# Cross-attention and a gated expert layer on one core: four late sums move from VectorE to ScalarE, one small load moves last, and all engine orders are rewritten

## The reference

```python
h  = layernorm(x)                                   # no affine part
q, k, v = h @ Wq.T + bq, ctx @ Wk.T + bk, ctx @ Wv.T + bv   # 16 heads of 32
p  = softmax(clip(q k^T / sqrt(32), -50, 50), masked)
d  = clip(rs, 0, 0.3) * ((p v) @ Wo.T + bo)         # rs: one number
x1 = x + layernorm(d) * gamma + beta
n  = layernorm(x1)
gate = top2 of softmax(n @ router.T)                # 8 experts
out  = x1 + sum_e gate_e * (silu(n @ down_e.T) @ up_e.T)    # 16 hidden features each
```

## Time and profile before

| | us |
|---|---|
| median of 3 runs | 186.54 (184.55 to 188.71) |
| profiled execution | 186.6 |
| its span, first to last instruction | 183.9 |
| TensorE busy in it | 171.8 |
| VectorE, ScalarE, GpSimd busy | 137.5, 113.4, 101.8 |
| DMA bytes read, written | 19.95 MB, 9.96 MB |

### The profile page before, as it was taken

The page is one execution under the profiler, slowest core; times in us unless marked ns, Lnnn a source line. Parts: engine busy times, 40 slices in busy tenths (PEclk is TensorE's granted clock), DMA queues, the critical chain, the costliest instruction groups (busy, mean ns, idle before and its releaser), DMA issues.

```text
span 183.9 us, 3557 instructions
## 1 busy us (share of the span) xinstructions
PE 171.8 (93%) x1212; PEld 126.2 (69%) x1212; DVE 137.5 (75%) x306; ACT 113.4 (62%) x231; POOL 101.8 (55%) x157
## 2 busy tenths in 40 slices
PE   7999779979998899999999999989999999999990
PEld 7486558846654378884888486666778598889860
DVE  3788498997999558998238584467898898773993
ACT  3038706984853875489986592769734787778410
POOL 5032089995837528999966984416133595364100
PEclk9999999999999999999999999999999999999999
DMA  6999995000157596455991526430409458000248
GB/s 168 354 384 300 399 250 207 4 0 4 62 150 279 136 284 172 124 179 204 302 215 67 173 59 197 148 95 18 114 18 329 127 221 235 4 2 0 86 176 309
DMA packets 18049, 30.13 MB, mean 164 GB/s; under 512 B 3056, under 2 KB 8176, under 8 KB 17776
## 3 DMA queue, kind: packets, MB, share of 16 engines
q1 hardware_dynamic: 18032, 29.92, 51.5%
HBM read 19.95 MB, written 9.96 MB: 163 GB/s over the span
## 4 chain that ended last, share of the span: by engine, by line
PE 44%; DVE 23%; DMA 13%; SPq 8%; issue 4%; POOL 3%; ACT 3%; DVEq 0%; ACTq 0%
PE ps L469 38%; DMA xs<-x 6%; DMA rz_scratch<-rz 3%; DVE xs L1223 3%; PE ps L574 3%; DVE stage L1147 3%; DVE ln_st L1231 3%; DVE hst_lo L1088 2%; DMA x_scratch<-x_turned 2%; PE ps L560 2%; DVE v_sb L1132 2%; POOL attt_lo L1509 2%; DMA wk<-rz_scratch 1%; SPq L360 1%; DVE wk L1157 1%
## 5 line engine op out<-in xcount | busy, mean ns | idle before, releaser
L1509 POOL TENSOR_TENSOR attt_lo<-wk,attt_hi 128x512 fp32r<-128x512 f32 x16 | 21.7, 1373 | 13.6 <-ACT attt_hi L801 13.5
L469 PE MATMUL ps<-hst_hi,wq_hi 128*128 128x512 f32 x64 | 26.2, 409 | 2.3 <-DVE hst_lo L1088 2.3
L469 PE MATMUL ps<-wo_hi,attt_hi 128*128 128x512 f32 x64 | 25.9, 405 | 0.2 <-POOL attt_lo L1509 0.2
L1505 POOL TENSOR_TENSOR xs<-xs,beta_bc 128x512 f32<-128x512 f32 x16 | 20.7, 1320 | 9.4 <-DMA beta_bc<-beta 8.1
L469 PE MATMUL ps<-hst_hi,wq_lo 128*128 128x512 f32 x64 | 25.3, 395 | 0.0
L469 PE MATMUL ps<-wo_hi,attt_lo 128*128 128x512 f32 x64 | 25.3, 395 | 0.0
L469 PE MATMUL ps<-wo_lo,attt_hi 128*128 128x512 f32 x64 | 25.3, 395 | 0.0
L469 PE MATMUL ps<-hst_lo,wq_hi 128*128 128x512 f32 x64 | 25.2, 394 | 0.0
L764 ACT ACTIVATE hs<-xs,ln_bias,ln_rstd 128x512 f32<-128x512 f32 x16 | 12.1, 807 | 11.5 <-POOL ln_bias L1497 11.5
L783 ACT ACTIVATE stage<-ps 128x1024 f32<-128x1024 f32 x16 | 15.9, 1025 | 5.3 <-PE ps L546 5.3
L1147 DVE TENSOR_SCALAR stage<-stage,exp_max 128x1024 f32<-128x1024 f32 x16 | 15.3, 959 | 5.1 <-ACT stage L783 5.1
(11 more groups left out here) (111 smaller groups left out, 387.6 us busy)
## 6 DMA issues: line engine op xcount, KB each, us to landing
wk<-rz_scratch SPq DMA_DIRECT2D x32, 128.0 KB, 2.8
out<-xs SPq DMA_DIRECT2D x16, 256.0 KB, 2.2
xs<-x SPq DMA_DIRECT2D x3, 1024.0 KB, 8.9
x_scratch<-x_turned SPq DMA_DIRECT2D x6, 512.0 KB, 2.6
x_turned<-x_scratch SPq DMA_DIRECT2D x24, 128.0 KB, 2.9
hs_scratch<-hs_turned SPq DMA_DIRECT2D x2, 1024.0 KB, 5.1
hs<-hs_scratch SPq DMA_DIRECT2D x8, 256.0 KB, 5.4
wk<-wk_t SPq DMA_DIRECT2D x4, 256.0 KB, 5.9
```

Of the source, the lines that this page charges most:

```text
L469: last = pe.matmul(dst, w, m, start=start and i == 0, stop=stop and i == n - 1, skip_group_check=unseen)
L1505: pool.tensor_tensor(xt, xt, beta_bc[:, :], ALU.add).then_inc(xb_ok, 1)
L1509: pool.tensor_tensor(attt_lo[:, :, c, :], att[:, c, :].rearrange("p (t n) -> p t n", t=NT), attt_hi[:, :, c, :].bitcast(F32), ALU.subtract ...
```

## The change

Four tiles, (2,1), (2,3), (3,1) and (3,2), get another way to their last sum. ScalarE copies x1 into the bank of the tile's experts (`experts_seed`, a use of kind `E` in `BANKS`), the three matmuls of `up` add to what is there, and ScalarE copies the sum back to SBUF (its own `finish`). VectorE no longer calls `finish` for them. The load of rs becomes `rs_load` and is issued as the last of the first loads; `residual_scale` stands later on VectorE. The other loads after `x1_load` come in another order, `load(3)` is issued before `hs_fetch(2)`, and the orders of all five engines and the uses of the banks are rewritten. No matmul, and no other computation, is added or taken away.

The part of the orders between those shown follows the same pattern: batch 0's experts (`down`, `hid_transpose`, `up`, `largest`, `gating`) come earlier on all engines, and `scores(1, 1)`, `sums(1, 1)` and `project(1, ...)` come later. On TensorE the sequence there is `project(0, 0)`, `(0, 1)`, `(0, 2)`, `sums(1, 0)`, `weigh(1, 0)`, `project(0, 3)`, `query(2, 0)`, `(2, 1)`, `down(0, 0)`, `(0, 1)`, `scores(1, 1)`, `query(2, 2)`, `scores(2, 0)`, `query(2, 3)`, `hid_transpose(0, 0)`, `sums(1, 1)`, `sums(2, 0)`, `up(0, 0)`, `(0, 1)`, `down(0, 2)`, `(0, 3)`, `weigh(1, 1)`, `scores(2, 1)`, `query(3, 0)`, `(3, 1)`, `hid_transpose(0, 1)`, `sums(2, 1)`, `project(1, 0)` to `(1, 3)`, `query(3, 2)`, `weigh(2, 0)`, `scores(3, 0)`, `weigh(2, 1)`, `query(3, 3)`, `down(1, 0)`, `(1, 1)`, `sums(3, 0)`, `scores(3, 1)`, `weigh(3, 0)`, `project(2, 0)`, `(2, 1)`, `sums(3, 1)`, `hid_transpose(1, 0)`, `project(2, 2)`, `down(1, 2)`, `(1, 3)`, `project(2, 3)`, `weigh(3, 1)`, `up(0, 2)`, `(0, 3)`, `hid_transpose(1, 1)`, `up(1, 0)`, `(1, 1)`, `down(2, 0)`, `(2, 1)`, `project(3, 0)`, `(3, 1)`, `hid_transpose(2, 0)`, `project(3, 2)`.

```diff
-    "K0 Q01 S02 S06 S10 Q13 W00 Q21 Q23 W12 S26 S30 W20 U01 U10 W33 U22 U33",
-    "K1 Q02 S03 S07 S11 S16 W03 S20 W10 W13 S27 S31 S34 W21 U02 W31 U20 U31",
-    "K2 Q03 S04 Q11 Q12 S17 Q20 S21 W11 Q30 S32 S35 W22 U11 U12 U23",
-    "K3 S00 S05 S12 S14 W01 Q22 S22 S24 Q31 S33 S36 W23 W30 U13 U30",
-    "h00 h02 Q00 S01 Q10 S13 S15 W02 S23 S25 Q32 Q33 S37 U00 U03 W32 U21 U32",
-    "V0 h11 m0 v02 v10 v13 v21 f01 f02 a00 v31 a01 v33 f20 a20 n30 f30 f32 a30",
-    "V1 h12 s00 v00 v03 v11 f00 s20 s21 v23 s30 v30 f11 v32 f12 f21 f22 n31 f31 f33 a31",
-    "h01 h03 h10 h13 s01 v01 s10 s11 v12 v20 v22 f03 s31 f10 a10 f13 a11 f23 n32 n33 a21",
+    "K0 Q02 Q03 Q10 S12 W03 Q22 Q23 S26 W11 S30 S34 W21 U03 W31 E31",
+    "K1 S00 S04 Q11 S13 Q20 S14 S20 U00 S27 W12 S31 S35 W22 U10 W32 U12 E32",
+    "K2 S01 S05 Q12 Q13 W02 S15 S21 U01 Q30 W13 S32 S36 W23 U11 W33 U13 U20 U22",
+    "K3 S02 S06 S10 W00 Q21 S16 S22 S24 Q31 Q32 S33 S37 E21 U30",
+    "h00 h02 Q00 Q01 S03 S07 S11 W01 S17 S23 S25 W10 Q33 W20 U02 W30 E23 U33",
+    "V0 h11 m0 v01 s10 f00 a00 f02 v13 v20 v23 s30 s31 f12 v33 f21 f22 n31 f31 f32 a30",
+    "V1 h12 s00 s01 v02 v10 f01 s20 v12 s21 v21 f10 v30 a10 f13 a11 f23 n32 a21",
+    "h01 h03 h10 h13 v00 v03 v11 s11 f03 a01 v22 f11 v31 v32 f20 a20 n30 f30 n33 f33 a31",
 )
 MOVED = ((0, 0), (0, 1), (1, 0), (1, 1), (2, 0), (2, 1))
+
+UP_ON_SCALAR = ((2, 1), (2, 3), (3, 1), (3, 2),)
 MOVED_HS = (2, 3,)
...
+e_seeded, e_full, e_free = sem("e_seeded"), sem("e_full"), sem("e_free")
...
+def rs_load():
     sp.dma_start(rs_raw[:, :], rs.broadcast_to([P, 1])).then_inc(rs_in, 16)
...
 def store(b, t):
-    sp.wait_ge(u_free, banks.count(f"U{b}{t}"))
+    if (b, t) in UP_ON_SCALAR:
+        sp.wait_ge(e_free, banks.count(f"E{b}{t}"))
+    else:
+        sp.wait_ge(u_free, banks.count(f"U{b}{t}"))
     sp.dma_start(out_tiles[:, bass.ds(NT * b + t, 1), :],
...
# SyncE's order
 small_load()
 x1_load()
+bv_load()
+experts_load()
+wo_load()
+load(2)
 gamma_load()
-wo_load()
 bo_load()
-experts_load()
-bv_load()
-load(2)
+rs_load()
 spread_out(0, 0)
 spread_in(0, 0)
 spread_out(0, 1)
# TensorE's up(b, t), then its order
-    dst = take(f"U{b}{t}")
-    passes(dst, three(hidt_hi[:, t, :], hidt_lo[:, t, :], up_hi[:, :], up_lo[:, :])
-           ).then_inc(u_full, 1)
+    weights = three(hidt_hi[:, t, :], hidt_lo[:, t, :], up_hi[:, :], up_lo[:, :])
+    if (b, t) in UP_ON_SCALAR:
+        pe.wait_ge(e_seeded, banks.count(f"E{b}{t}"))
+        passes(bank(f"E{b}{t}"), weights, start=False, unseen=True).then_inc(e_full, 1)
+    else:
+        passes(take(f"U{b}{t}"), weights).then_inc(u_full, 1)
 values(0)
+keys(0)
 values(1)
-keys(0)
-keys(1)
 hs_transpose(0, 0)
 hs_transpose(0, 1)
-values(2)
+keys(1)
 keys(2)
-values(3)
 hs_transpose(0, 2)
 hs_transpose(0, 3)
+values(2)
+values(3)
+query(0, 0)
 keys(3)
-query(0, 0)
 query(0, 1)
 query(0, 2)
+scores(0, 0)
 query(0, 3)
 hs_transpose(1, 0)
 hs_transpose(1, 1)
-scores(0, 0)
 hs_transpose(1, 2)
+scores(0, 1)
 hs_transpose(1, 3)
 expert_means()
-scores(0, 1)
+sums(0, 0)
 query(1, 0)
-sums(0, 0)
+weigh(0, 0)
 sums(0, 1)
 query(1, 1)
-weigh(0, 0)
-scores(1, 0)
 query(1, 2)
 weigh(0, 1)
+scores(1, 0)
 query(1, 3)
-sums(1, 0)
-scores(1, 1)
-weigh(1, 0)
 project(0, 0)
-sums(1, 1)
 project(0, 1)
...
 project(3, 0)
 project(3, 1)
-hid_transpose(1, 1)
 hid_transpose(2, 0)
 project(3, 2)
+project(3, 3)
+up(1, 2)
 down(2, 2)
 down(2, 3)
-project(3, 3)
+up(1, 3)
 x1_transpose(3, 0)
 x1_transpose(3, 1)
 x1_transpose(3, 2)
 down(3, 0)
 down(3, 1)
+hid_transpose(2, 1)
 x1_transpose(3, 3)
 down(3, 2)
 down(3, 3)
-up(1, 2)
-up(1, 3)
-hid_transpose(2, 1)
 up(2, 0)
 up(2, 1)
 hid_transpose(3, 0)
# ScalarE: new functions, then the end of its order
+def experts_seed(b, t):
+    before = banks.before(f"E{b}{t}")
+    act.wait_ge(x1_ok, NT * b + t + 1)
+    act.wait_ge(freeing[before[0]], banks.count(before))
+    act.copy(bank(f"E{b}{t}"), xs[:, NT * b + t, :]).then_inc(e_seeded, 1)
+
+def finish(b, t):
+
+    act.wait_ge(e_full, banks.count(f"E{b}{t}"))
+    act.copy(xs[:, NT * b + t, :], bank(f"E{b}{t}")).then_inc(e_free, 1)
+
 def projected_squares(b, t):
...
+projected_squares(3, 2)
 x1_out(2, 3)
-projected_squares(3, 1)
-hid_hi(1, 1)
-hid_hi(2, 0)
-x1_squares(3, 0)
-projected_squares(3, 2)
+x1_squares(3, 1)
+experts_seed(3, 1)
+x1_squares(3, 2)
+projected_squares(3, 3)
+experts_seed(3, 2)
 down_scaled(2, 2)
-x1_squares(3, 1)
 down_scaled(2, 3)
 hidden_tanh(2, 1)
+x1_out(3, 0)
 exp_logits(2, 1)
-x1_squares(3, 2)
-projected_squares(3, 3)
-x1_out(3, 0)
 x1_out(3, 1)
 x1_out(3, 2)
 x1_squares(3, 3)
 down_scaled(3, 0)
 down_scaled(3, 1)
-x1_out(3, 3)
 hidden_tanh(3, 0)
 exp_logits(3, 0)
+x1_out(3, 3)
 down_scaled(3, 2)
+hid_hi(2, 1)
 down_scaled(3, 3)
 hidden_tanh(3, 1)
-hid_hi(2, 1)
 exp_logits(3, 1)
 hid_hi(3, 0)
+finish(2, 1)
+finish(2, 3)
 hid_hi(3, 1)
+finish(3, 1)
+finish(3, 2)
# VectorE's order: start and end
-clean_finite(1)
 tile_stats(0, 0)
 tile_stats(0, 1)
+clean_finite(1)
+tile_stats(0, 2)
+tile_stats(0, 3)
 clean_marks(2)
-tile_stats(0, 2)
 clean_limited(2)
+hs_lo(0, 0)
 clean_finite(2)
 clean_marks(3)
-tile_stats(0, 3)
-hs_lo(0, 0)
+clean_limited(3)
 hs_lo(0, 1)
-clean_limited(3)
+clean_finite(3)
 wq_low(0)
-clean_finite(3)
 wq_low(1)
+hs_lo(0, 2)
+hs_lo(0, 3)
 wq_low(2)
 wq_low(3)
+tile_stats(1, 0)
 mask_limits()
-residual_scale()
-tile_stats(1, 0)
-hs_lo(0, 2)
-hs_lo(0, 3)
 tile_stats(1, 1)
 tile_stats(1, 2)
 tile_stats(1, 3)
-centre_wo(0)
-centre_wo(1)
-centre_wo(2)
 value_blocks(0)
 value_blocks(1)
 tile_stats(2, 0)
 tile_stats(2, 1)
 tile_stats(2, 2)
+residual_scale()
+centre_wo(0)
+centre_wo(1)
+centre_wo(2)
+clip(0, 0)
+clip(0, 1)
 hs_lo(1, 0)
 hs_lo(1, 1)
-clip(0, 0)
 hs_lo(1, 2)
 hs_lo(1, 3)
...
 scaled(3, 0)
 residual(3, 0)
-hid_lo(1, 1)
 hid_lo(2, 0)
 scaled(3, 1)
 residual(3, 1)
 scaled(3, 2)
 residual(3, 2)
+finish(1, 2)
+scaled(3, 3)
+residual(3, 3)
+finish(1, 3)
 largest(2, 1)
 gating(2, 1)
-scaled(3, 3)
-residual(3, 3)
 largest(3, 0)
 gating(3, 0)
-finish(1, 2)
+hid_lo(2, 1)
 largest(3, 1)
-finish(1, 3)
-hid_lo(2, 1)
+finish(2, 0)
 gating(3, 1)
 hid_lo(3, 0)
-finish(2, 0)
-finish(2, 1)
+finish(2, 2)
 hid_lo(3, 1)
-finish(2, 2)
-finish(2, 3)
 finish(3, 0)
-finish(3, 1)
-finish(3, 2)
 finish(3, 3)
```

423 lines of the change are left out of this document (217 added, 206 removed).

## The result

The changed kernel took **191.34 us** (median of 4 runs, 189.45 to 194.77) beside 186.7 for the kernel before: ratio 1.027, interval 1.020 to 1.035. That it is slower is clear of the noise; whether by two per cent, these runs alone leave just open. The same file, timed again in a later session (`after_again`, 190.20 to 194.74), had a median of 193.23 beside 185.79; the ratio of the plain medians is 1.025 in the first session and 1.040 in the second. Forecast were 184.0, a range of 181.4 to 187.8, and 0.05 for slower.

A forecast was written before the change was run, and what follows sets the result against it. TensorE, busy 171.8 of 183.9 us, was taken as the bound, so only its waits counted; the terms summed to -2.55 us, a span of 181.35 and, with 2.7 us around it, 184.0 us, range 181.4 to 187.8.

The forecast's parts named there:

- Middle: Batches 2 and 3: TensorE waits of 0.67, 0.16 and 0.16 us go, -1.0 us (-1.0 to +1).
- the new wait of +0.7: At batch 3, down(2, 0) waits for x1_out(2, 0), which ScalarE does behind four att_hi: +0.7 us.
- Loads and turned tiles: load(3) ahead of hs_fetch(2) costs nothing, up to +2 us if that fetch is slow.
- The head: First batch: the 2.27 us wait before query(0, 0) goes, about 0.8 us of new idling comes, net -1.5 us.
- -1.5, +0.2 and -0.25: Terms up to project(0, 0): the head, rs loaded last (longer wait before hs_transpose(1, 3)), and the first attention.
- First attention: Before project(0, 0): waits of 0.78 and 0.7 us go, a wait of 1.0 to 1.2 comes, net -0.25 us.
- The four sums and the tail: Behind the last matmul: VectorE has one sum left instead of three, net -0.7 us (-1.2 to +0.8).
- Waits are only displaced: Rival: work pulled forward takes cover from what it passes, only the tail's 0.7 us stays, 185.9 us; chance 0.24.
- rs decides: Rival: rs, loaded last, lands late and holds VectorE at residual_scale, 188.5 us at bo's 12.8 us; chance 0.09.

The follow-up runs named there:

- middle_alone: Kernel before with its first 47 us kept, all that follows in the changed kernel's order and banks, every sum on VectorE: ratio 1.046 to the kernel before.
- gpsimd_quiet: Changed kernel with GpSimd's six add_beta of batches 0 and 1 moved behind wo_low(0) to (2) and batch_power(2): ratio 1.066 to the kernel before.
- vector_sums: Changed kernel with the four late sums back on VectorE, without ScalarE's copies in and out: ratio 1.034 to the kernel before.
- waits_covered: Changed kernel with clip(1,1), project(2,2), down(2,2) and down(2,3) moved earlier to take away three TensorE waits: ratio 1.044 to the kernel before.
- wo_first_covered: The edit of waits_covered, plus VectorE's centre_wo(0) to (2) ahead of tile_stats(2,*), on the changed kernel: ratio 1.027 to the kernel before.
- clips_back: Changed kernel with VectorE's clip(0,0) and clip(0,1) put back behind hs_lo(1,0) and hs_lo(1,2): ratio 1.039 to the kernel before.
- mid_attention: Kernel before with only attention, projection and residual orders from 47 us to x1_turn(1,3) as changed, batch 0's experts left in place: ratio 1.067.

## Why the prediction was wrong, point by point

**The step that failed: "Middle", put at -1.0 us, and the new wait of +0.7.** With the 0 for the loads the forecast had -0.3 us for all behind `project(0, 0)` up to the last matmul. It measured +6.2 and +7.7. Of the latter 6.5 us are TensorE waits (7.5 against 1.0), and 1.3 us are no waits above 0.15 us. By the distances between starts 0.9 us of these lie in and just behind the groups of `down`; why stays open. The waits of after_again there are owed to VectorE (4.2 us: 1.05 to `clip`, 1.7 in two to `product`, 1.4 in two to `scaled`), ScalarE (1.6 us in three, `x1_out` and `down_scaled`) and GpSimd (1.5 us in two, `hs_lo` of batches 2 and 3). I looked for waits that go, checked one new chain, and found one wait. The forecast's +0.7 for `down(2, 0)` was 0.29. That the new middle order costs this is shown by middle_alone. Which of its moves do it is not shown: no half of it and no single wait could be made out as the cause.

**"Loads and turned tiles: nothing", with "some 3 us in hand".** `tile_stats(3, 0)` stood 2.79 us (3.08 in after_again) for load(3), with `clip(1, 1)` behind it: `sums(1, 0)` waited 0.76 and 1.04, and `query(2, 0)` 0.77 and 0.78 for `hs_lo`. It came at 74.1 in after_again, not at 71. The margin was as large as the wait.

**The head.** `query(0, 0)` began at 20.84 (forecast 21 to 22.5). rs landed 8.6 us after its issue at 23.51, and `residual_scale` began at 32.17 after 0.28 us (31 to 33): right. (The 12.8 us that bounded it above were those of bo, a load of 256 KB and not a small one; rs has 0.5 KB.) The forecast let VectorE's piece end at 39.0, TensorE wait 1.3 and `project(0, 0)` start near 58: after_again shows 38.83, 1.26 and 58.60, and its head gained 1.8 us where -1.5, +0.2 and -0.25 had been added up. In the profile of after they are 42.79, 4.03 and 64.57. What was left out is that the piece moves into GpSimd's adds, because beta now lands 7 us later (30.72, before 23.53). The slow subtraction stood in the trace of the kernel before; GpSimd's adds and VectorE's first two `centre_wo` there:

```profile
23.53 5.03 POOL L1505 TENSOR_TENSOR xs<-xs,beta_bc 128x512 f32<-128x512 f32 x4 [8.15 <-DMA beta_bc<-beta]
...
27.50 1.34 DVE L1243 TENSOR_SCALAR xs<-xs,w_mv 128x512 f32<-128x512 f32 x1
...
29.77 0.49 DVE L1243 TENSOR_SCALAR xs<-xs,w_mv 128x512 f32<-128x512 f32 x1
```

The one begun during an add took 1.34 us, the one behind the adds 0.49. The count that ended at 39.0 holds only where all three are short; that they were in after_again is luck of the start times. The Trainium skill (SBUF — State Buffer, "Who interferes with whom") says that the two engines share a pair of ports, which VectorE takes in its two-port modes (`tensor_scalar` is among the instructions that can enter them), and that "whoever issues first gets the shared pair for the whole instruction". The rows agree: in gpsimd_quiet 0.49 us alone and 1.39 when begun 0.19 us into a GpSimd instruction, in after_again 0.51 when begun 0.19 us ahead of one, which then took 1.47 us.

**First attention** at -0.25: right in kind, 0.35 us of waiting where 1.0 to 1.2 was counted.

**The four sums and the tail** at -0.7: -1.3 and -1.4 measured, of which vector_sums gives the sums 0.5; middle_alone, with the new order and every sum on VectorE, ends 3.9 us behind its last matmul, so the rest is the order's. ScalarE's copies took 588 ns out and 586 in, as said.

**The rivals.** "Waits are only displaced" (185.9) named the mechanism, but ended it at nothing lost. "rs decides", the rival for slower, is refuted by the profiles: rs was waited for 0.28 us in after and not at all in after_again. (Those 0.28 us did count, but through the order of starts beside GpSimd, which no rival had.) None had the middle losing: cover taken from work that is pulled forward was priced at one place, and in after_again TensorE waited at eleven behind it.

## What to carry to other kernels

Where the bound engine is already busy in all of a stretch, as TensorE from 64 to 100 us of the kernel before (columns as above; 36.00 of 36.00 us),

```profile
64.00:100.00 36.00, 36.00 (x209) 27.51 (x208) 25.27 (x45) 27.00 (x55) 26.69 (x37) 1.00 0.66 193
```

a new order of all engines can only add waits there: walk each engine's queue against the others, and don't look only for the old waits that vanish. Parts of two hand-written orders don't combine: of six mixtures, the four with a changed middle cost 4.6 to 6.7 per cent. Where an f32 VectorE subtraction or clip moves, look at what GpSimd does at that time.

## What the runs showed of the hardware

A `tensor_scalar` of 128x512 f32 took 0.49 us with GpSimd idle. Six of them in the heads of after, gpsimd_quiet and the kernel before took 1.29 to 1.41 us when begun 0.14 to 0.30 us into one of GpSimd's `tensor_tensor`s. In after_again two begun 0.09 and 0.19 us ahead of GpSimd's next instruction, in the last 0.2 us or so of the one before, took 0.49 and 0.51 us, and that next instruction took 1.54 and 1.47 us instead of 1.28. One program's executions fall into either pattern from starts 0.4 us apart.

All nine TensorE waits of 3.08 to 7.03 us had a stretch at granted clock 0.50 (1.2 GHz) during them or just behind. Of eight waits between 1.89 and 2.55 us four had one: 1.89 in waits_covered, 2.01 in gpsimd_quiet, 2.07 in wo_first_covered, 2.55 in clips_back. Four had none: 2.07 in waits_covered, 2.27 in the kernel before, 2.37 in mid_attention, 2.44 in vector_sums. The length of the single wait does not tell them apart.
